# Causal attention: diagonal probability blocks cleared by GpSimd, value products two steps behind the scores

## The reference

```
scores = einsum('bhqd,bhkd->bhqk', Q, K) / sqrt(8)      # 16 heads of 8 features
scores = where(causal, scores, -1e10)                   # a query sees keys up to its own position
att = softmax(scores, axis=-1)
y = einsum('bhqk,bhkd->bhqd', att, V)                    # then the output projection
```

## Time and profile before

| | us |
|---|---|
| Median of 3 runs | 1765.23 |
| Lowest, highest | 1761.93, 1765.70 |
| Profiled execution, its own time | 1763.04 |
| Its span | 1760.8 |
| TensorE, VectorE, ScalarE, GpSimd busy | 1211.1, 992.7, 629.3, 554.7 |

### The profile page before, as it was taken

How to read it: one execution, slowest core, us unless ns; L and a number is a source line. 1 busy time by engine, 2 the same in 40 slices (tenths; PEclk the granted TensorE clock), 3 DMA queues, 4 the chain that set the end, 5 groups by cost and what they waited for, 6 DMA issues and landing times. The chain is left out here.

```text
span 1760.8 us, 26686 instructions
## 1 busy us (share of the span) xinstructions
PE 1211.1 (69%) x9140; PEld 799.2 (45%) x9214; DVE 992.7 (56%) x2284; ACT 629.3 (36%) x989; POOL 554.7 (32%) x627
## 2 busy tenths in 40 slices
PE   4525977959635059804788998999799997412991
PEld 2313856839525049702244443444344443312991
DVE  6865555655426126434776776777577771631662
ACT  4632221212111023202165665666476666101330
POOL 2434013040026747723013102400240000374772
PEclk9766988969755569955599999999899999555996
DMA  1439611020120133160000001001000100213325
GB/s 45 156 148 386 270 37 60 0 95 0 36 63 29 53 104 99 53 187 6 7 19 7 8 19 33 12 9 43 8 7 8 31 7 13 62 53 94 96 68 161
DMA packets 109057, 114.06 MB, mean 65 GB/s; under 512 B 8720, under 2 KB 90512, under 8 KB 108048
## 3 DMA queue, kind: packets, MB, share of 16 engines
q1 hardware_dynamic: 96608, 91.98, 16.6%
q0 software_dynamic: 9216, 19.02, 3.2%
q10 hardware_dynamic: 3120, 1.57, 0.3%
HBM read 49.34 MB, written 59.02 MB: 62 GB/s over the span
## 5 line engine op out<-in xcount | busy, mean ns | idle before, releaser
L1834 DVE TENSOR_REDUCE att_mx<-att_ps 128x1 f32<-128x512 f32 (+3 forms) x768 | 405.4, 555 | 163.8 <-PE att_ps L1727 123.7
L1608 ACT ACTIVATE att_prob<-att_ps 128x1024 f32<-128x1024 f32 (+3 forms) x384 | 300.1, 812 | 218.9 <-PE att_ps L1739 160.6
L1724 PE MATMUL att_ps<-att_kT,att_q1T 128*128 128x512 bf16 (+3 forms) x712 | 236.6, 345 | 34.2 <-DVE att_mx L1834 18.0
L1736 PE MATMUL att_ps<-att_q2T,att_kT 128*128 128x512 bf16 (+3 forms) x750 | 200.3, 330 | 4.2 <-ACT att_prob L1608 1.8
L1724 PEld LDWEIGHTS att_ps<-att_kT,att_q1T 128*128 128x128 bf16 x768 | 74.4, 98 | 235.6 <-DVE att_mx L1834 182.6
L978 POOL DMA_INDIRECT sides<-moe_ys,moe_back_i x160 | 153.2, 957 | 87.5 <-issue 47.3
L1750 PE MATMUL att_pso<-att_prob,att_v 128*32 128x512 f32 (+3 forms) x1536 | 165.4, 503 | 1.5
L972 POOL DMA_INDIRECT slots<-moe_rows,moe_place_i x128 | 123.1, 961 | 59.7 <-issue 38.4
L1503 POOL CAST att_qm_rows<-att_nm 128x32 bf16<-128x32 f32 x48 | 15.5, 323 | 390.7 <-DVE att_nm L1843 386.5
L1727 PE MATMUL att_ps<-att_mask,att_identb 128*128 128x128 bf16 x512 | 115.5, 228 | 2.3 <-DVE att_mx L1834 1.5
L1071 PE MATMUL moe_ps_t<-moe_ident,moe_xs 128*128 128x128 f32 x160 | 27.0, 289 | 115.1 <-DMA moe_xs<-slots 115.1
(11 more groups left out here) (283 smaller groups left out, 2447.7 us busy)
## 6 DMA issues: line engine op xcount, KB each, us to landing
slots<-fw_zeros SPq DMA_DIRECT2D x2, 5200.0 KB, 30.6
moe_xs<-slots SPq DMA_DIRECT2D x16, 650.0 KB, 4.5
sides<-fw_zeros SPq DMA_DIRECT2D x2, 4096.0 KB, 35.2
moe_side<-sides SPq DMA_DIRECT2D x16, 512.0 KB, 6.3
tok<-prep_tok SPq DMA_DIRECT2D x4, 1536.0 KB, 5.4
turned<-prep_tT SPq DMA_DIRECT2D x4, 1536.0 KB, 8.8
fw_tok<-tok SPq DMA_DIRECT2D x4, 1536.0 KB, 10.8
fw_Tkv<-turned SPq DMA_DIRECT2D x4, 1024.0 KB, 7.1
```

Source lines behind the costliest of these rows:

```text
L1608: nc.scalar.activation(prob[(2 * n + pair) % 4][:, :, 0:size], ps2[pair][:, :, 0:size], ACT.Exp, scale=SCORE_SCALE).then_inc(exp_done, 1)
L1724: last = nc.tensor.matmul(out[:, 0:size], q1T[t % 2][:, j * P:(j + 1) * P], kT[t][h][:, 512 * c:512 * c + size], start=True, stop=not diag ...
L1736: last = nc.tensor.matmul(ps2[pair][:, h, 0:size], kT[t][2 * pair + h][:, i * P:(i + 1) * P], q2T[t % 2][:, first:first + size], start=Tru ...
L1834: nc.vector.reduce_max(mx[:, c, j, h:h + 1], ps1[(n * QUAD + h) % 2][:, 0:size], AX.X).then_inc(max_done, 1)
```

## The change

The product that adds the mask in `exp_step` goes. Instead GpSimd sets the probabilities of future keys to zero in the first 128 columns of each diagonal block, two heads in one `affine_select`; the value product of a diagonal step waits for this (semaphore `cleared`) in place of the exponentials. Value products run two steps behind, with six buffers `prob`. GpSimd's work in a slot is dealt out over the steps. The normalization of the tiles moves from GpSimd to VectorE, in two halves. Several uses of `psm` have other places. The maxima pass keeps its masks.

```diff
+        BEHIND = 2
-        prob = [sb(f"prob{s}", [P, 2, 512]) for s in range(4)]
+        prob = [sb(f"prob{s}", [P, 2, 512]) for s in range(2 * (BEHIND + 1))]
+        DIAGONAL = [n for n, (c, i) in enumerate(EXP_STEPS) if i >= 4 * c]
-        COMMON = {(1, "end"): "o1", (5, "end"): "k", (6, "end"): "q1", (7, "end"): "o0", (10, "end"): "q2"}
-        PREP = {(3, "mid"): "x0", (4, "mid"): "x1", (6, "mid"): "qk0", (7, "mid"): "qk1", (8, "mid"): "qk2", (9, "mid"): "qk3"}
+        COMMON = {(2, "end"): "o1", (5, "end"): "k", (6, "end"): "q1", (7, "end"): "o0", (10, "end"): "q2"}
+        PREP = {(4, "mid"): "x0", (4, "end"): "x1", (5, "mid"): "qk0", (6, "mid"): "qk1", (7, "mid"): "qk2", (8, "mid"): "qk3"}
-        OUTPUT = {(2, "end"): "y0", (3, "mid"): "y1", (3, "end"): "out0", (4, "mid"): "out1"}
+        OUTPUT = {(3, "end"): "y0", (4, "mid"): "y1", (4, "end"): "out0", (5, "mid"): "out1"}
...
+            def clear_future(G, n, pair):
+                wait(pool, exp_done, G * (2 * STEPS) + (2 * n + pair) + 1 + BUFFERS)
+                block = prob[(2 * n + pair) % len(prob)][:, :, 0:P]
+                nc.gpsimd.affine_select(block, block, [[0, 2], [1, P]], ALU.is_ge, 0.0, base=0, channel_multiplier=-1).then_inc(cleared, 1)
...
             def slot(S):
-                if S.prep:
-                    rsqrt(S.b + 1)
-                if S.more2:
-                    ...                                   # copy_queries
-                if S.more1:
-                    stack_maxima(S.G + 1, (S.t + 1) % QUADS)
-                if S.prep:
-                    wait(pool, misc_free, 1 + S.count("qk3") + 1)
-                    for k, done in ((0, q_split), (1, k_split)):
-                        rotate(nc.gpsimd, k)
-                        for n in range(3):
-                            last = split(nc.gpsimd, k, n)
-                        last.then_inc(done, 1)
-                if S.t == 1:
-                    add_output_bias(S.b)
+                next_batch = S.t == 2 and S.more2
+                for n in range(STEPS):
+                    if n in DIAGONAL:
+                        clear_future(S.G, n, 0)
+                        clear_future(S.G, n, 1)
+                    if S.prep and n == 1:
+                        rsqrt(S.b + 1)
+                    if S.more2 and n == 5:
+                        ...                               # copy_queries
+                    if S.t == 1 and n == 4:
+                        add_output_bias(S.b)
+                    if S.more1 and n == 7:
+                        stack_maxima(S.G + 1, (S.t + 1) % QUADS)
+                    if S.prep and n == 9:
+                        wait(pool, misc_free, 1 + S.count("qk3") + 1)
+                        rotate(nc.gpsimd, 0)
+                    if S.prep and n > 9:
+                        split(nc.gpsimd, 0, n - 10)
+                    if next_batch and n == 0:
+                        split(nc.gpsimd, 0, 2).then_inc(q_split, 1)
+                    if next_batch and n == 1:
+                        rotate(nc.gpsimd, 1)
+                        split(nc.gpsimd, 1, 0)
+                    if next_batch and n == 2:
+                        split(nc.gpsimd, 1, 1)
+                    if next_batch and n == 3:
+                        split(nc.gpsimd, 1, 2).then_inc(k_split, 1)
...                                                       # ScalarE: stack_keys wholly in step 4, copy_output one step later
                     last = nc.tensor.matmul(ps2[pair][:, h, 0:size], kT[t][2 * pair + h][:, i * P:(i + 1) * P], q2T[t % 2][:, first:first + size],
-                                            start=True, stop=(i < 4 * c))
-                    if i >= 4 * c:
-                        last = nc.tensor.matmul(ps2[pair][:, h, 0:P], identb[:], mask[:, 1], start=False, stop=True)
+                                            start=True, stop=True)
...
-                pe.wait_ge(exp_done, G * (2 * STEPS) + 2 * (n + 1) + BUFFERS)
+                if n in DIAGONAL:
+                    pe.wait_ge(cleared, G * (2 * len(DIAGONAL)) + 2 * (DIAGONAL.index(n) + 1))
+                else:
+                    pe.wait_ge(exp_done, G * (2 * STEPS) + 2 * (n + 1) + BUFFERS)
...
+            def normalize(batch, half):                   # VectorE: both halves in step 3 of a preparing slot
+                wait(dve, rstd_done, batch + 1)
+                for j in range(4 * half, 4 * half + 4):
+                    last = nc.vector.tensor_scalar(xn[:, j], xb[:, j], mv[:, j, 0:1], rstd[:, j:j + 1], ALU.subtract, ALU.mult)
+                last.then_inc(xn_done, 1)
```

More of the change, by code:

```diff
@@ L1441, in _ @@
             with sp.Fori(0, BATCH - 1) as b:
-                wait(sp, xn_done, b + 1)
+                wait(sp, xn_done, 2 * b + 2)
                 sp.dma_start(xb[:], batch(x_in, b + 1)).then_inc(x_loaded, 16)
@@ L1485, in rsqrt @@
                 pool.drain()
[L1486 to L1490, removed]
+                nc.gpsimd.tensor_tensor(rstd[:], vareps[:], negh[:], ALU.pow).then_inc(rstd_done, 1)
+            def clear_future(G, n, pair):
+                wait(pool, exp_done, G * (2 * STEPS) + (2 * n + pair) + 1 + BUFFERS)
+                block = prob[(2 * n + pair) % len(prob)][:, :, 0:P]
+                nc.gpsimd.affine_select(block, block, [[0, 2], [1, P]], ALU.is_ge, 0.0, base=0, channel_multiplier=-1).then_inc(cleared, 1)
             def copy_queries(G, t):
@@ L1615, in slot @@
                     exponential(S.G, n, 1)
-                    if n == 0 and not S.first:
+                    if n == BEHIND - 1 and not S.first:
                         copy_output(S.G - 1, 1)
-                    if n == 0 and S.t == 0:
+                    if n == BEHIND - 1 and S.t == 0:
                         act.wait_ge(misc_free, 1 + S.start)
                         place_values(S.b)
-                    if n == 4:
+                    if n == 3 + BEHIND:
                         copy_output(S.G, 0)
@@ L1633, in slot @@
                         stack_queries(2).then_inc(q_stacked, 1)
+                    if S.t == 2 and S.more2 and n == 4:
                         act.wait_ge(k_split, S.b + 2)
                         stack_keys(0)
-                    if S.t == 2 and S.more2 and n == 4:
                         stack_keys(1)
@@ L1750, in value_step @@
                     last = nc.tensor.matmul(pso[32 * h:32 * h + 32, first:512], v1[:, i * HEADS + QUAD * t + h, :],
-                                            prob[(2 * n + h // 2) % 4][:, h % 2, 0:512 - first], start=(i == 0), stop=(i == 4 * c + 3))
+                                            prob[(2 * n + h // 2) % len(prob)][:, h % 2, 0:512 - first], start=(i == 0), stop=(i == 4 * c + 3))
                 last.then_inc(pv_done, 1)
             def serve(S, use):
-                if use == "x0":
-                    pe.wait_ge(xn_done, S.b + 2)
+                if use in ("x0", "x1"):
+                    pe.wait_ge(xn_done, 2 * (S.b + 1) + int(use[1]) + 1)
                 if use == "k" and S.t == 2:
@@ L1781, in slot @@
                         serve(S, S.uses[n, "mid"])
-                    if n >= 1:
-                        if n == 1 and S.t == 0:
+                    if n >= BEHIND:
+                        if n == BEHIND and S.t == 0:
                             pe.wait_ge(v_placed, S.b + 1)
-                        value_step(S.G, S.t, n - 1)
+                        value_step(S.G, S.t, n - BEHIND)
                     elif not S.first:
-                        value_step(S.G - 1, (S.t - 1) % QUADS, STEPS - 1)
+                        value_step(S.G - 1, (S.t - 1) % QUADS, STEPS - BEHIND + n)
                     if quad:
@@ L1822, in _ @@
                 slot(S)
-            value_step(QUADS * BATCH - 1, QUADS - 1, STEPS - 1)
+            for n in range(STEPS - BEHIND, STEPS):
+                value_step(QUADS * BATCH - 1, QUADS - 1, n)
             for use in TAIL_USES:
@@ L1890, in slot @@
                         consume(use, S.count(use), S.t, S.b - 1)
+                    if S.prep and n == 3:
+                        normalize(S.b + 1, 0)
                     if quad:
@@ L1900, in slot @@
                         statistics(S.b + 1)
+                    if S.prep and n == 3:
+                        normalize(S.b + 1, 1)
             nc.vector.engine_nop().then_inc(exp_done, BUFFERS)
@@ L1909, in _ @@
             nc.vector.memset(k_rows[:, :, 24:27], 1.0)
+            normalize(0, 0)
+            normalize(0, 1)
             dve.wait_ge(weights_in, 7 * 16)
```

13 lines of the change are left out of this document (7 added, 6 removed).

## The result

The changed kernel takes 1778.5 us (median of 4 runs, 1774.9 to 1780.3), the kernel before 1765.3: ratio 1.0076, 95% interval 1.0056 to 1.0097. It is slower by 13 us where 1757, 8 us faster, was forecast; 1778.5 lies just beyond the range's upper end. A second set on another occasion gave 1.0073 (1.0056 to 1.0089). The profiled execution took 1777.7 us with a span of 1776.0.

The account below looks back on a forecast made before the run. Steps were taken as held in turn by TensorE's issue times and VectorE's reductions. Slot gains -16, normalization -6, the preparation's place +16 and head 0 summed to -6 us on 1763.0, forecasting 1757 us, range 1742 to 1778.

Parts of the forecast that it names:

- normalization to VectorE: Preparing slots: eight normalization instructions leave GpSimd for VectorE, ending TensorE's wait for them; gain 2 us a slot, 6 for three.
- shared access: VectorE beside GpSimd's work: a cast took 1.33 us against 0.43, but PSUM reductions were not slowed; nothing added for them.
- the plain slots: Slots without next-batch preparation: fall from 34.2 to 32.3 us, 2.0 us less; five such slots give 10 us.
- Masks: Removed score mask products on TensorE count only in steps 1, 8, 9 and 10: 0.9 us a slot.
- the shifted value products: Value products one step later: no work removed, but redistributed; step 1 falls to 1.7 us, step 2 grows to 3.2.
- The larger of two sums: Pricing rule: a step lasts as long as the larger of TensorE's issue times and VectorE's reductions, 2.75 us for four.
- the preparation's place: Quad-2 slots: clears between GpSimd's rotation and splits delay the key parts; net +5.2 us a slot, +16 us in all.
- 12c - 0.55: ScalarE's stall in step 4 of each quad-2 slot, c being one clear's time in us; 4.85 us at c = 0.45.
- the clear: GpSimd's zeroing of 256 elements on 128 partitions: 0.45 us taken, bounds 0.3 to 1.6; no cost in plain slots.
- the head: First batch's normalization at the stage's start: VectorE ends it at 795.9 where GpSimd ended at 795.78; no change.
- (b): Rival: dearer clears hold the keys in quad-2 slots; slower from 0.63 us a clear, 1769 at 0.8; chance 0.22.
- (c): Rival: VectorE's reductions are slowed beside the clears, 1.7 us a slot, kernel 1778; chance 0.06.

## Why the prediction was wrong

**The step that failed: normalization to VectorE.** I had "2 us a slot, 6 us for three" as a gain, with bounds of 0 and 4. Measured it is a loss of 2 us a slot, 6 for three. Step 3, forecast at 4.5 us, took 6.85. The mechanism of contention was in my prediction as *shared access*, with the cast of 1.33 us beside GpSimd, and I dismissed it because the reductions read PSUM. That was right for reductions and wrong for the eight instructions that the change itself brought to VectorE, which read and write SBUF; "the new normalizations may pay; that is inside the bounds above" did not ask what GpSimd would be doing at that moment. In its new order it does the bias and the copy exactly there. With both moved away step 3 takes 3.65 us and the preparing slots 46.3. That is close to my sum (48.5 less 2), but partly by luck: step 3 is then shorter than forecast, while steps 4 and 5 cost 1.1 and 1.3 us more than before where I had 0.5 and 0.9. Nor did the gain hang on the move to VectorE, as I had it: with the normalization on GpSimd the slots take 45.7.

**Mis-sized: the plain slots.** Masks 0.9 us a slot, measured 0.5 to 0.6; the shifted value products 1.1, measured 0.5. The plain slot came to 33.3 and not 32.3, and the total over the plain, quad-0, quad-3 and last slots is 7.8 us against 16. Step 1 fell to 2.08 and not 1.7, step 5 to 2.89 and not 2.6, step 3 rose from 2.25 to 2.45. Steps 8 to 10, which were to win 0.5 us, stayed as they were (8.22 and 8.18 us together): the run without masks has 7.98 there, the run two steps behind 8.42, so what the masks win the later value products take back. The larger of two sums assumes that in a step only one engine counts. That an engine also waits while the other has its turn would explain the rest; no run shows it by itself.

**Right: the preparation's place.** Forecast +5.2 us a quad-2 slot, measured +4.2. Of this the stall of the key stacks was forecast at 4.85; the formula 12c - 0.55 gives 4.3 with the clear's 0.407, and they waited 3.5. Leaving the clears out took 4.8 off, doubling them put 6.1 on, and keeping masks in those six steps took 4.9 off.

**Right: the clear**, 0.407 us against 0.45 taken and 0.3 to 1.6 as bounds; free in plain slots, as the run without them shows. **Right: the head**; the rows were ready at 798.0, 15.7 us after the stage's first instruction, against 16.4 before. **Missed:** 2.0 us behind the last exponential, of which the later value product shows 0.65; the rest is open.

In the sum: -7.8 in place of -16, +5.8 in place of -6, +12.6 in place of +16, +2 in place of 0: +12.6 against 13 measured. Another 2 us of the distance to 1757 are the forecast's base: it took the 6 us off the profiled execution of 1763.0, not off the median of 1765.3, from which the same sum gives 1759. Of the rivals none was it. (b), a dear clear, gives the slower side by the quad-2 slots alone, and would have needed 0.63 us; (c) named the right neighbours but the wrong instruction; that its figure was 1778 is luck, for the reductions stayed at 0.689 us.

## What to carry to other kernels

When work moves from GpSimd to VectorE, look at what GpSimd will run at the same moment: an elementwise instruction between SBUF tiles can be held for the whole length of its neighbour, as here 0.34 us became 2.39. Small instructions on an in-order queue cost little by themselves and delay all that stands behind them; keep them off it where a chain is just in time, as the masks left on TensorE in six steps did for 4.9 us a quad-2 slot. And price a step held by two engines by taking a part away on the chip: sums of issue times gave twice the gain.

## What the runs showed of the hardware

VectorE's tensor_scalar of 128 f32 elements between SBUF tiles takes 0.34 us alone. Beside a GpSimd instruction it ends 0.08 us behind it: 0.51 us beside a clear of 0.41, 0.84 beside a copy of 0.82, 2.39 beside an add of 2.34. One begun 0.24 us into a clear, with 0.16 left of it, took 0.35 and lost nothing. The add took 2.34 us with VectorE held beside it and 2.35 without: here the wait was VectorE's alone. The other way round was seen only with doubled clears: three clears that began 0.13 us behind such a VectorE instruction took 0.47 us in place of 0.41. Reductions of 512 columns that read PSUM stayed at 0.689 us throughout. The Trainium skill (Advanced Engine Details and Errata, VectorE Performance Modes) says that VectorE's second SBUF port is shared with GpSimd, so that its two-port instructions and GpSimd's interfere or block each other, and lists source and destination in SBUF among the conditions for these modes. The runs agree that one blocks the other, 0.34 us becoming 2.39; in which mode the instructions ran no run shows.

An `affine_select` of 128 x 256 f32 took 0.407 us in the mean of 255, below the 0.62 of a cast of 512 and far below the 0.8 of iota's rate.
